# The last four slots of a chunked linear-attention layer: a hand-written order for them, an earlier start for the weight signs of the next stage, and the last fold moved

## The reference, cut to what matters

```python
h = _layernorm(x) * (1 + ca) + sa
# attention: 32 heads, 8 groups, D = 128, chunks of 128 tokens
scores  = einsum('bhnid,bhnjd->bhnij', qc, kc)
y_intra = einsum('bhnij,bhnjd->bhnid', scores * decay, xc)
cstates = einsum('bhnjd,bhnje->bhnde', k_dec, xc)       # scanned over chunks
y_inter = einsum('bhnid,bhnde->bhnie', qc * exp(G), prev)
y = (y_intra + y_inter) / rms * gnorm_w * silu(gate)
x = x + ga * (y @ Wo.T)
h = _layernorm(x) * (1 + cb) + sb
w = wscale * sign(weight) + wbias                       # 512 x 512
x = x + gb * einsum('bsk,nk->bsn', h, w)
```

## Time and profile before

| | us |
|---|---|
| median of 3 runs | 1577.71 (1576.15 to 1586.4) |
| the profiled execution, whole | 1575.66 |
| its span in the trace | 1573.8 |
| PE busy | 1263.4 (80%) |
| DVE busy | 1005.2 (64%) |
| POOL busy | 747.7 (48%) |
| ACT busy | 627.5 (40%) |

### The profile page before, as it was taken

The page is one execution under the profiler, slowest core; times in us unless marked ns, Lnnn a source line. Parts: engine busy times, 40 slices in busy tenths (PEclk is TensorE's granted clock), DMA queues, the critical chain, the costliest instruction groups (busy, mean ns, idle before and its releaser), DMA issues. The chain is left out here.

```text
span 1573.8 us, 18591 instructions
## 1 busy us (share of the span) xinstructions
PE 1263.4 (80%) x6071; PEld 889.5 (57%) x6071; DVE 1005.2 (64%) x1724; ACT 627.5 (40%) x1174; POOL 747.7 (48%) x750
## 2 busy tenths in 40 slices
PE   2768999999999999999999999667989999951000
PEld 0447776776776777777777777556754333330000
DVE  4644655655655656655656666666577888537888
ACT  0333333333433424434333433235317777734223
POOL 2236756655756657657756756566210012041007
PEclk8789999999999999999999999879968999965555
DMA  5120122222222221221121120310565310000001
GB/s 180 53 64 21 57 72 68 60 74 68 60 74 68 61 67 48 60 75 45 56 74 47 61 68 20 94 68 1 113 101 84 50 51 2 2 1 0 0 0 54
DMA packets 71137, 87.53 MB, mean 56 GB/s; under 512 B 6922, under 2 KB 40874, under 8 KB 70467
## 3 DMA queue, kind: packets, MB, share of 16 engines
q1 hardware_dynamic: 69170, 83.63, 19.6%
q10 hardware_dynamic: 1872, 2.72, 0.5%
HBM read 78.54 MB, written 7.52 MB: 55 GB/s over the span
## 5 line engine op out<-in xcount | busy, mean ns | idle before, releaser
L1169 DVE TENSOR_REDUCE nm<-banks 128x2 f32<-128x1024 f32 x128 | 152.2, 1220 | 35.4 <-PE banks L738 34.8
L1635 POOL TENSOR_TENSOR sw<-sw,sinT 128x512 f32<-128x512 f32 x80 | 103.1, 1289 | 141.8 <-ACT sw L1360 141.8
L1409 ACT ACTIVATE yTh<-yF 128x512 fp32r<-128x512 f32 x64 | 40.4, 632 | 319.7 <-DVE yF L1026 319.7
L1647 POOL TENSOR_TENSOR dec<-gb,gcol 128x512 f32<-128x512 f32 x64 | 70.3, 1099 | 196.4 <-DVE Sd L992 188.8
L1517 ACT ACTIVATE Pb<-banks 128x512 f32<-128x512 f32 x256 | 135.0, 601 | 52.6 <-PE banks L759 52.3
L588 PE MATMUL banks<-st,qt 128*128 128x128 f32 x384 | 79.9, 291 | 52.8 <-DVE Sd L992 27.6
L536 PE MATMUL banks<-hTh,wgh 128*128 128x512 f32 x256 | 120.4, 470 | 0.0
L964 DVE SCALAR_TENSOR_TENSOR gs<-tg,banks 128x512 f32<-128x512 f32 x64 | 44.0, 688 | 115.8 <-ACT tg L1367 115.8
L536 PE MATMUL banks<-hTh,wqh 128*128 128x512 f32 x256 | 107.9, 422 | 0.0
L616 PE MATMUL banks<-woh,yTh 128*128 128x512 f32 x256 | 104.1, 406 | 1.6 <-DVE yTl L1029 1.6
L536 PE MATMUL banks<-hTh,wql 128*128 128x512 f32 x256 | 101.4, 396 | 0.0
(11 more groups left out here) (305 smaller groups left out, 3421.0 us busy)
## 6 DMA issues: line engine op xcount, KB each, us to landing
gb<-g_scr SPq DMA_DIRECT2D x64, 256.0 KB, 3.5
raw<-in_wmod SPq DMA_DIRECT2D x40, 256.0 KB, 2.7
raw<-in_wo SPq DMA_DIRECT2D x32, 256.0 KB, 2.8
raw<-in_wq SPq DMA_DIRECT2D x31, 256.0 KB, 2.7
raw<-in_wg SPq DMA_DIRECT2D x31, 256.0 KB, 2.7
qsT<-q_scr SPq DMA_DIRECT2D x24, 256.0 KB, 6.7
q_scr<-hl SPq DMA_DIRECT2D x32, 128.0 KB, 4.8
mt<-mods_scr SPq DMA_DIRECT2D x12, 256.0 KB, 5.0
```

The costliest lines, as they stand in the source:

```text
L1169: ve.tensor_reduce(nm[:, b, i, p:32:16], pairs[z_][:, :].rearrange("p (g t) -> p g t", g=2), AX.X, ALU.max, negate=True).then_inc(*v_nm.up ...
L1635: po.tensor_tensor(s_[:, :], s_[:, :], sinT[:, :], ALU.mult).then_inc(*g_rope.up("sin", kind, t, n))
L1647: po.tensor_tensor(dec[:, :, :], gb[s % 2][:, :, :], bc(gcol[:, t % 2, heads(t), n], 2, 128), ALU.subtract).then_inc(*g_dec.up("sub", s))
```

## The change

It does six things.

1. Slots 60 to 63 have a function of their own, `last_slot`. In it `scores` of the next slot stands right behind the outputs of this one, and the work of the next stage stands ahead of `outputs` (`beside_outputs`). On POOL `prep2` is split: `xc` ahead of the power, `qt` and `xdd` behind the state. The `yn` of a slot stands ahead of its state.
2. `w_values` is cut in four: the greater-than pass at the end of slot 58, the sign pass in two halves at the end of slot 59, scale and bias in slot 60. The weight's load moves from slot 59 to slot 57. `fwt` moves to other memory (the key and value weights), so that `norm` of batch 1 no longer waits for the weight's transposes, and the loads of `xin` 4 to 7, which lie there, wait for them.
3. The four norms of batch 0 are in slots 63 and just behind, and its `turn_h` are all in `last_folds`, behind the outputs of slot 63.
4. `fold_a` of slot 63 stands between the second and third `turn_h`, and its `fold_b` between the fourth and the first `ffn`. Before, both stood between `ffn` tiles.
5. `key_cols_` stands ahead of these `turn_h`, and all four residuals of batch 1 are in `last_folds`.
6. The norms of batch 1 are spread between the `ffn` tiles.

```diff
-    fwt = over(8, "fwt", [128, 4, 512])
+    fwt = over(64, "fwt", [128, 4, 512])
...
+        def w_values(self, part):
+            ve = self.e
+            if part == 0:
+                ve.wait_ge(*d_f("fb"))
+                ve.wait_ge(*p_proj("v", 15, 0))
+                ve.tensor_scalar(fsb[:, 0, :], fsb[:, 0, :], -1.0, None, ALU.mult).then_inc(*v_fw.up("neg"))
+                ve.tensor_scalar(flat(fwt), flat(fwr), 0.0, None, ALU.is_gt).then_inc(*v_fw.up("gt"))
...
-            if of == "f" and b == 1:
-                ac.wait_ge(*p_fw(3))
...
+            if part < 0:
+                sp.wait_ge(*p_proj("q", 15, 1))
+                sp.dma_start(fwr[:, :, :], I["fw"].rearrange("(t p) k -> p t k", p=128)).then_inc(*d_f.up("fw"))
...
+                sp.wait_ge(*p_fw(3))
                 for i in range(4, 8):
                     sp.dma_start(xin[i][:, :], x_in[i]).then_inc(*d_x[i].up("xin"))
...
+    def beside_outputs(E, s):
+
+        if s == NSLOT - 4:
+            E.tables(0, None), E.tables(1, None)
+            E.w_values(3)
+            for k in range(3):
+                E.w_turn(k, E.bank())
+        elif s == NSLOT - 3:
+            E.w_turn(3, E.bank())
+            E.col_turn(E.bank())
+            E.residual("f", 0), E.residual("f", 1)
+        elif s == NSLOT - 2:
+            E.tables(2, E.bank()), E.tables(3, E.bank())
+            E.residual("f", 2), E.residual("f", 3)
+            E.moments("f", 0)
+        else:
+            E.moments("f", 1), E.norm("f", 0), E.moments("f", 2), E.norm("f", 1), E.moments("f", 3)
+
+    def last_slot(E, s):
+
+        ahead = s + 1 < NSLOT
+        if ahead:
+            E.prep(s + 1)
+        E.fold_a(s - 1)
+        if ahead:
+            E.prep_exp(s + 1)
+        beside_outputs(E, s)
+        E.outputs(s)
+        E.norm_a(s)
+        if ahead:
+            E.scores(s + 1)
+            E.prep2(s + 1, ("xc",))
+        E.norm_pow(s)
+        if s + 2 < NSLOT:
+            E.load_gb(s + 2)
+        if ahead:
+            E.start_loads(s - NSLOT + 5)
+        E.norm_b(s)
+        E.state(s)
+        if ahead:
+            E.prep2(s + 1, ("qt", "xd"))
+        E.fold_b(s - 1)
...
     def last_folds(E):
 
+        last = NSLOT - 1
+        E.norm("f", 2), E.norm("f", 3)
         E.key_cols_()
+        turn(E, "f", 0, 0, E.bank())
+        turn(E, "f", 0, 1, E.bank())
+        E.fold_a(last)
+        turn(E, "f", 0, 2, E.bank())
+        turn(E, "f", 0, 3, E.bank())
+        for i in (4, 5, 6):
+            E.residual("f", i)
         E.conv(8), E.conv(9)
+        E.moments("f", 4)
+        E.fold_b(last)
+        E.loop_end()
+        E.moments("f", 5)
+        E.residual("f", 7)
         E.ffn(0, E.bank())
...
+        E.ffn(1, E.bank())
+        E.norm("f", 6)
+        E.moments("f", 7)
         E.ffn(2, E.bank())
-        E.moments("f", 7), E.norm("f", 6)
+        E.norm("f", 7)
         E.ffn(3, E.bank())
...
+        for s in range(NSLOT - 4, NSLOT):
+            last_slot(E, s)
         last_folds(E)
```

More of the change, by code:

```diff
@@ L1037, in fold_b @@
                 ve.tensor_tensor(acc[:, i, :], acc[:, i, :], banks[bO][:, :], ALU.add).then_inc(*v_acc.up(s))
-        def w_values(self):
+        def w_values(self, part):
             ve = self.e
[L1042 to L1051, removed]
+            if part == 0:
[3 more added lines that the diff above has]
+                ve.tensor_scalar(flat(fwt), flat(fwr), 0.0, None, ALU.is_gt).then_inc(*v_fw.up("gt"))
+            elif part < 3:
+                a, b = fwr[:, 2 * part - 2:2 * part, :], fwt[:, 2 * part - 2:2 * part, :]
+                a, b = (x.rearrange("p t n -> p (t n)") for x in (a, b))
+                ve.wait_ge(*v_fw("gt"))
+                ve.scalar_tensor_tensor(out=b, in0=a, scalar=0.0, in1=b, op0=ALU.is_lt, op1=ALU.subtract).then_inc(*v_fw.up("sign", part))
+            else:
+                ve.wait_ge(*v_fw("sign", 2))
+                for t in range(4):
+                    ve.tensor_scalar(fwt[:, t, :], fwt[:, t, :], fsb[:, 0, t:t + 1], fsb[:, 1, t:t + 1], ALU.mult,
+                                     ALU.add).then_inc(*v_fw.up("w", t))
         def w_turn(self, k, bk):
@@ L2059, in first_pieces @@
             E.piece("g", 0, n), (yield)
[L2061 to L2079, removed]
@@ L2324, in layer0_loop @@
             E.split()
-        for s in range(NSLOT):
+        for s in range(NSLOT - 4):
             t, n = s // 4, s % 4
[L2327 to L2330, removed]
+            more = t + 1 < NSLOT // 4
             E.scores(s)
-            if ahead:
-                E.prep(s + 1)
+            E.prep(s + 1)
             if s:
@@ L2338, in layer0_loop @@
             E.outputs(s)
-            for _ in range(beside[0]):
-                front.step()
             E.norm_a(s)
-            if ahead:
-                E.prep_exp(s + 1)
+            E.prep_exp(s + 1)
             E.norm_pow(s)
@@ L2347, in layer0_loop @@
             E.state(s)
-            for _ in range(beside[1]):
-                front.step()
-            if s + 2 < NSLOT:
-                E.load_gb(s + 2)
-            if NSLOT - 5 <= s < NSLOT - 1:
-                E.start_loads(s - NSLOT + 5)
-            if s == NSLOT - 1:
-                E.residual("f", 4), E.residual("f", 5)
+            E.load_gb(s + 2)
+            if s == NSLOT - 7:
+                E.start_loads(-1)
+            if s == NSLOT - 5:
+                E.start_loads(0)
             E.norm_b(s)
@@ L2363, in layer0_loop @@
                 E.turn_v(t + 1)
-            for _ in range(beside[2]):
-                front.step()
-            if ahead:
-                E.prep2(s + 1)
+            E.prep2(s + 1)
             if s:
@@ L2373, in layer0_loop @@
                 E.split()
-            for _ in range(beside[3]):
-                front.step()
-        front.rest()
+            if s == NSLOT - 6:
+                E.w_values(0)
+            if s == NSLOT - 5:
+                E.w_values(1), E.w_values(2)
+        E.scores(NSLOT - 4)
+        for s in range(NSLOT - 4, NSLOT):
+            last_slot(E, s)
         last_folds(E)
```

59 lines of the change are left out of this document (21 added, 38 removed).

## The result

The changed kernel took **1571.61 us** (median of 20 runs, 1566.32 to 1582.17), the kernel before 1580.98 beside it (median of 20, 1572.02 to 1591.2). The ratio is 0.9945, with a 95% interval of 0.9928 to 0.9963: 8.7 us less, between 5.8 and 11.4. It lies inside the range that was given, and it is a gain of less than 1%. The forecast had 11.2 less. The 1571.61 lies above the 1561.5 to 1568 that had the chance of 0.55.

The account below looks back on a forecast made before the run. The prediction took a chain of latencies from slot 60 to batch 1's transposes as the bound. A 3.9 us earlier first `ffn` tile and 11.6 instead of 19.0 after it gave -11.2, so 1564.5, taken as 1565; range 1558.5 to 1572.5.

Parts of the forecast that it names:

- Slots 57 to 59: nothing: Early weight load and passes ahead of slot 59's `Sd` cost nothing, with 1 us of cover; at most 1.4 us.
- Slots 60 to 63: Outputs move from 992.3 to 1001.2, 1005.7 to 1009.2, 1026.2 to 1020.6 and 1042.3 to 1032.6.
- `ffn(0)`: First `ffn` tile of batch 0 starts at 1051.3 instead of 1055.2, with slot 63's product already done.
- Batch 1's transposes: After four `ffn` tiles, they start at 1062.9 instead of 1074.15; `key_cols_` and key splits cost nothing.
- The term with two ends: DVE and POOL slowing each other in slots 61 to 63: none taken, or about 2.5 us a slot, 7.5 in all.
- Contention on every slot: Rival: DVE and POOL slow each other in every slot, gain only 3.7 us, so 1572; chance 0.15.
- PE warm over the short gaps: Rival: gaps ahead of slots 62, 63 and the last product keep the clock, 5.2 us less, 1559 to 1560; chance 0.15.
- The slow rival: PE stays at the low clock through it all, 3 us slower, 1578 to 1579; chance 0.05.
- The order binds elsewhere: Rival: late `gb` or `xin` holds POOL, or tile 7's norm is late, 3 us or more; 1568 to 1570; chance 0.10.

Follow-up runs that it names:

- e7_work_behind: Changed kernel with the next stage's work behind, not ahead of, the outputs of slots 60 to 63: 1570.56 us in one run.
- e5_muls_first: Changed kernel with residual products 0 and 1 ahead of the fourth weight transpose in slot 61: 1560.82 us in one run.
- e6_best: Changed kernel, key splits in middle, residual products 0 and 1 before fourth weight transpose, decay exponentials behind squares, residuals 2 and 3 ending slot 62: 1561.63 us, ratio 0.9873.

## Why the prediction held, and where it failed

**Slots 57 to 59: nothing. Right.** `Sd` of slot 59 ends at 987.2, more than 1 us ahead of the outputs at 988.56.

**Slots 60 to 63: right** (18.1, 25.2, 36.9, 49.7 for 18.0, 26.0, 37.4, 49.4). In slot 60 that is in part luck, as two errors cancel. The sign pass took 2.35 for both halves where I took 3.2. POOL had no instruction beside it. But I read 1.9 for twelve transposes "at the low clock" from a row whose clock was 0.78. At 0.50 they take 2.6 until the outputs start. Slot 61 came 0.8 early: the outputs and the state product of slot 60 took 2.3 to the next scores, where I took 3.1. In slot 62 `qt` does not end the wait, as it should by the forecast. It ended at 1025.21, while PE was busy until 1025.50 with the transposes of `yn` and the table matmuls (L670). But `yn` had waited for POOL's power, behind two adds and `xc`, so POOL's queue did set it. In slot 63 the forecast had the chain that was measured: `gb` landed 39.8 behind the outputs of slot 59 for the 39.7 forecast (issued earlier, and 4.29 on the way for 3.7), the decay was ready at 41.7 for 41.4, the sums behind two exponentials and two table copies at 46.0 for 45.2. What I did not ask is whether the squares have to stand behind them.

**`ffn(0)`: right**, 67.2 for 68.1. The product of slot 63 took 4.45 to `ffn(0)`, for 4.8, behind 3.46 idle for 3.4.

**"Batch 1's transposes": this is the step that failed, in size.** It gave 11.6 from `ffn(0)` on, and 15.3 were measured. The failing sentence is that `key_cols_` and the key splits lie beside PE's last product and cost nothing. They do lie beside PE's product, and past its end, and nothing on PE waits for them. But on DVE the moments of tiles 4 to 7 and the sum of slot 63's product stand behind them, and then the norms, which end on the path. The forecast has that product added 3.3 after its end; 6.8 were measured (1055.79 to 1062.59), and 2.9 in the kernel without the splits here. Taking them away gave 11.6 and a stretch of 78.3. "The two are level" named two arrivals that would tie, PE's tiles and the norm of tile 7, and I did not sum DVE's queue on the second with all that stands in it.

**The term with two ends.** DVE and POOL do slow each other, as said, but I priced it in slots 61 to 63 only, where it was small: `qt` took 1.29 in the chain and `xc` 1.04, both near the lower end. It came in the tail, where three adds of POOL meet the last two of three products and three splits of DVE, all with both inputs in SBUF. The trace shows both engines slower there: POOL's adds took 1.69 each (5.06 for three, 1.24 for one later in the chain), and DVE's split of 128x512 took 1.78 in place of 0.69. The Trainium skill ("GPSIMD Engine Reference", section Specifications) has GpSimd's SBUF interfaces as shared with VectorE, with contention where VectorE's instruction has two SBUF inputs; the trace agrees.

**The rivals.** Contention on every slot: no, slots 62 and 63 were on time. PE warm over the short gaps: no, outputs of slot 62 began at 0.76 and the product of slot 63 followed its 3.46 of idle at the low clock. The slow rival: no, the granted clock was 1.00 from `ffn(0)` to batch 1's transposes. The order binds elsewhere: yes, in its second half. It names a late norm of tile 7 by 3 us or more, and that norm came 2.9 late. Its cause was not named.

**The sum and the range.** 1565 does not follow from its own sum. The profiled execution less 11.2 is 1564.5, and a median 2 us above it gives 1566.5. The 1571.61 lies 6.6 above 1565. Some 2.5 are gain that did not come, 1.5 are this sum, and 3.3 are no part of the change: the kernel before had a median of 1577.71 in the three runs shown and of 1580.98 in the twenty. (These three give 7.3; the ratio and the difference of the medians are 0.7 apart.) The time lies inside the range, but in the part that the range has for its rivals. Right are the waits of slots 60 to 63 and the size of the gain to within 3 us.

**Where the gain came from.** Of 8.4 us the early weight passes bring 2.3 (undone) to 3.4 (alone), and the fold ahead of the `ffn` tiles 2.5. The inner order of the slots takes 1.1 back. What is left, some 4, would be the other parts of the change; that is a remainder and was not run by itself. The place of the next stage's work ahead of the outputs is not it (e7_work_behind); which slot each piece stands in may be. The key splits cost 4 in the changed kernel. They stood in the same function before, where the wait ahead of batch 1's transposes was 1.06, ended by the norm; what they cost there was not run.

## What to carry to other kernels

When a wait is closed by reordering, sum the queue of every engine up to the next join with all that stands in it, work without a deadline included: an instruction that "lies beside" one engine stands in front of something on its own. When a price is read from a matmul row, read the granted clock of that row too. Price contention wherever two engines have SBUF work at once, not only where the change was aimed. And where a whole execution swings by more than the term, measure a stretch between two fixed points of the program in both traces.

## What the runs showed of the hardware

**The same idle time, and two clocks.** Ahead of the outputs of slot 57, before any moved instruction, PE stands idle for 2.96 or 2.97 us in all 13 traces. In the profiled execution of the kernel before, the clock did not drop (PE timeline, then the window):

```profile
955.00 0.49 PE L588 MATMUL banks<-st,qt 128*128 128x128 f32 x2 [2.97 <-DVE Sd L992]
955.33 0.39 PE L589 MATMUL banks<-xc,Sd 128*128 128x128 f32 x2
```

```profile
954.00:961.00 7.00, 6.00 (x33) 4.93 (x34) 4.25 (x7) 3.73 (x7) 4.96 (x5) 1.00 0.00 0
```

In that of the changed kernel, at the same place, it did:

```profile
957.64 0.79 PE L588 MATMUL banks<-st,qt 128*128 128x128 f32 x2 [2.97 <-DVE Sd L992]
958.23 0.64 PE L589 MATMUL banks<-xc,Sd 128*128 128x128 f32 x2
```

```profile
957.00:964.00 7.00, 6.36 (x22) 5.14 (x23) 3.95 (x6) 3.44 (x6) 5.16 (x5) 0.54 0.00 0
```

And in the second trace of the kernel before it did too:

```profile
959.84 0.80 PE L588 MATMUL banks<-st,qt 128*128 128x128 f32 x2 [2.97 <-DVE Sd L992]
```

A pair of matmuls takes 0.39 at a granted clock of 1.00 and 0.64 at 0.54, and the outputs of slot 58 follow those of slot 57 after 15.5 in the one case and 18.3 in the other: 2.8 us. Of the 13 traces, 3 kept the clock (the first of the kernel before, e5_muls_first and e6_best) and 10 lost it. The earlier load of the weight has no part in it: it goes out behind this wait (at 965.60 in the changed kernel), and there are traces on both sides without it and with it. What decides was not found. What follows the stretch to the end takes 493 to 496 us in eight traces and 498 to 501 in five, and each of the two kernels has one of either kind. The outputs of slot 59 start between 983.0 and 998.1, and the twenty runs of the kernel before spread over 19 us. So a gain of 8 us is not read from one execution of each, but from a stretch or from many runs.

**DVE and POOL slow each other where both read two SBUF inputs.** DVE's 128x512 split took 0.69 alone and 1.78 beside POOL's adds, 2.6 times as long. POOL's adds took 1.69 each beside DVE's products and splits and 1.24 later, 1.4 times as long.
